# Routed experts: gate and up products as three FP32r products of split operands, with four result buffers

## What is computed

```python
logits = x @ gate_weight.T                   # x: 2048 x 256, 64 experts
...                                          # softmax, best 6 experts of 3 of 8 groups
buf[slot] = x[tok]                           # 64 experts x 96 slots x 256
g = einsum('ech,emh->ecm', buf, Wg)          # Wg, Wu: 64 x 176 x 256
u = einsum('ech,emh->ecm', buf, Wu)
out = einsum('ecm,ehm->ech', silu(g) * u, Wd)
y = sum(out[slot] * topk_w)  +  shared expert
```

## Time and profile before

| | |
|---|---|
| median of 3 runs | 1696.71 us (1686.70 to 1700.94) |
| span of the profiled execution | 1695.7 us, granted TensorE clock 0.932 on average |
| busy, share of the span | TensorE 85%, VectorE 63%, GpSimd 46%, ScalarE 44% |
| moved by DMA | 145.50 MB, mean 86 GB/s |

### The profile page before, as it was taken

How to read it: one execution, slowest core, us unless ns; L and a number is a source line. 1 busy time by engine, 2 the same in 40 slices (tenths; PEclk the granted TensorE clock), 3 DMA queues, 4 the chain that set the end, 5 groups by cost and what they waited for, 6 DMA issues and landing times. The chain is left out here.

```text
span 1695.7 us, 39494 instructions
## 1 busy us (share of the span) xinstructions
PE 1441.4 (85%) x14334; PEld 990.9 (58%) x14334; DVE 1075.4 (63%) x2743; ACT 750.3 (44%) x1786; POOL 773.8 (46%) x741
## 2 busy tenths in 40 slices
PE   6879999448889996888999478877899999998799
PEld 3556656414545554455566356654677777777687
DVE  6852222457876564783222388876998888874888
ACT  5533333254555633553333311125776666752322
POOL 4453332763320000454333466606998888973000
PEclk9989999569999998899999788888999999999899
DMA  8309995631110002514999232200000000000000
GB/s 265 98 14 267 284 266 150 204 96 38 38 38 1 1 1 67 152 40 123 280 296 259 73 87 84 78 4 13 3 16 3 12 7 3 16 3 3 10 19 22
DMA packets 92664, 145.50 MB, mean 86 GB/s; under 512 B 25032, under 2 KB 52528, under 8 KB 92512
## 3 DMA queue, kind: packets, MB, share of 16 engines
q1 hardware_dynamic: 62816, 93.06, 19.1%
q0 software_dynamic: 15360, 37.77, 7.7%
q10 hardware_dynamic: 14336, 12.59, 2.7%
HBM read 122.39 MB, written 18.87 MB: 83 GB/s over the span
## 5 line engine op out<-in xcount | busy, mean ns | idle before, releaser
L2298 POOL TENSOR_TENSOR sb_m_prob<-sb_m_prob,sb_m_rinv 128x512 f32<-128x512 f32 x256 | 260.1, 1041 | 44.6 <-DVE sb_m_rinv L2348 40.8
L1272 POOL DMA_INDIRECT sb_c_rows<-slot_rows,sb_slot x192 | 192.1, 1000 | 102.7 <-issue 51.2
L2228 ACT ACTIVATE sb_m_prob<-m_ps_s,sb_m_nmax 128x512 f32<-128x512 f32 x256 | 173.8, 683 | 125.8 <-DVE sb_m_nmax L2354 125.2
L1106 POOL DMA_INDIRECT e_xn<-xn_rows,sb_table x128 | 117.7, 920 | 209.6 <-PE e_ps_x L1184 197.2
L1255 DVE TENSOR_TENSOR sb_e_h<-sb_e_sg,e_ps_gu 96x176 f32<-96x176 f32 x128 | 42.6, 333 | 256.5 <-ACT sb_e_sg L1231 256.5
L1193 PE MATMUL e_ps_gu<-e_wgu,sb_e_xT 128*96 128x352 f32 x512 | 178.1, 470 | 17.0 <-ACT sb_e_xT L1225 15.6
L2354 DVE TENSOR_REDUCE sb_m_nmax<-m_ps_s 128x1 f32<-128x512 f32 x256 | 163.8, 681 | 28.1 <-PE m_ps_s L2132 25.7
L2362 DVE STREAM_TRANSPOSE sb_m_pT<-sb_m_prob 128x1024 f32<-128x1024 f32 x128 | 157.5, 1232 | 0.0
L2145 PE MATMUL m_ps_v<-sb_m_pT,sb_m_lat_rows 32*64 32x128 f32 x8192 | 136.1, 275 | 4.6 <-issue 3.8
L2131 PE MATMUL m_ps_s<-sb_m_latT_high,sb_m_qa 128*128 128x512 f32 x256 | 125.5, 490 | 16.0 <-ACT sb_m_prob L2228 15.9
L2145 PEld LDWEIGHTS m_ps_v<-sb_m_pT,sb_m_lat_rows 32*64 32x64 f32 x8192 | 120.2, 131 | 27.8 <-issue 27.4
(11 more groups left out here) (280 smaller groups left out, 3076.4 us busy)
## 6 DMA issues: line engine op xcount, KB each, us to landing
e_wgu<-wgu SPq DMA_DIRECT2D x128, 352.0 KB, 4.9
e_wdn<-wdn SPq DMA_DIRECT2D x128, 192.0 KB, 4.7
slot_rows<-sb_e_y ACTq DMA_DIRECT2D x128, 96.0 KB
xn_rows<-e_xn SPq DMA_DIRECT2D x16, 256.0 KB, 2.2
sb_c_rows<-slot_rows,sb_slot POOLq DMA_INDIRECT x192, 2.8
sb_x<-x SPq DMA_DIRECT2D x4, 512.0 KB, 5.4
e_xn<-xn_rows,sb_table POOLq DMA_INDIRECT x128, 5.3
sb_g_zm<-wqT SPq DMA_DIRECT2D x1, 2048.0 KB, 9.1
```

The source lines that it names most:

```text
L1106: pool.indirect_dma_start(x, None, k.xn_rows[:, :], bass.IndirectOffsetOnAxis(ap=k.table[:, e:e + 1], axis=0))\
L1272: pool.indirect_dma_start(rows[u][j][:, :], None, k.slot_rows[:, :], bass.IndirectOffsetOnAxis(ap=k.slot[:, n, j:j + 1], axis=0))\
L2228: act.activation(prob[s % 4][:, hh, :], ps_s[j % 3][:, :], ACT.Exp, bias=nmax[s % 2][:, hh:hh + 1], accum_out=rsum[s % 2][:, hh:hh + 1]).t ...
L2298: pool.tensor_tensor(part, part, rinv[s % 2][:, hh:hh + 1].to_broadcast([P, T]), ALU.mult)\
```

## The change

In the routed experts, the tokens and the gate/up weights are each split into a high part (rounded to FP32r by a ScalarE copy) and a low part (what remains, rounded to FP32r, by a VectorE subtraction). The product becomes three products for each half of the features, high x high, high x low and low x high. The weights of expert s+1 are split in step s, into three buffers of pairs; the wait for the loaded weights goes from TensorE to ScalarE. SyncE may load over a `wgu` buffer once its low part is made. The results `y` have four buffers and four semaphores.

```diff
--- before.py
+++ after.py
@@ -1112,23 +1112,25 @@
 
 
 
-    U, GA, LAG = AHEAD, 4, 3
+    U, GA, LAG, YB, WB = AHEAD, 4, 3, 4, 3
     got = [k.sem(f"e_tokens_got{u}") for u in range(GA)]
     w_got = [k.sem(f"e_weights_got{u}") for u in range(U)]
-    xT_raw, xT_ready = k.sem("e_xT_psum_ready"), k.sem("e_xT_ready")
+    xT_raw, xT_high, xT_low = k.sem("e_xT_psum_ready"), k.sem("e_xT_high_ready"), k.sem("e_xT_low_ready")
+    w_high, w_low = k.sem("e_weight_high_ready"), k.sem("e_weight_low_ready")
     gu_ready, act_ready, h_ready = k.sem("e_gate_up_ready"), k.sem("e_silu_ready"), k.sem("e_hidden_ready")
     hT_raw, hT_ready = k.sem("e_hT_psum_ready"), k.sem("e_hT_ready")
     dn_ready, y_ready = k.sem("e_down_ready"), k.sem("e_y_ready")
-    y_stored = [k.sem(f"e_y_stored{u}") for u in range(2)]
+    y_stored = [k.sem(f"e_y_stored{u}") for u in range(YB)]
     with ExitStack() as ctx:
         sb, ps = scoped(nc, ctx)
         x = k.gathered
-        xT = [sb(f"e{r}_xT{u}", [P, DC, CAP]) for u in range(2)]
+        xTs = [[sb(f"e{r}_xT_{part}{u}", [P, DC, CAP], F32R) for part in ("high", "low")] for u in range(2)]
         wgu, wdn = k.wgu, k.wdn
+        ws = [[sb(f"e{r}_w_{part}{u}", [P, DC, 2 * M0], F32R) for part in ("high", "low")] for u in range(WB)]
         sg = [sb(f"e{r}_sg{u}", [CAP, M0]) for u in range(2)]
         h = [sb(f"e{r}_h{u}", [CAP, M0]) for u in range(2)]
         hT = [sb(f"e{r}_hT{u}", [MH, 2, CAP]) for u in range(2)]
-        y = [sb(f"e{r}_y{u}", [CAP, D]) for u in range(2)]
+        y = [sb(f"e{r}_y{u}", [CAP, D]) for u in range(YB)]
         ps_x = [ps(f"e{r}_ps_x{u}", [P, DC, CAP]) for u in range(2)]
         ps_gu = [ps(f"e{r}_ps_gu{u}", [CAP, 2 * M0]) for u in range(2)]
         ps_h = [ps(f"e{r}_ps_h{u}", [MH, 2, CAP]) for u in range(2)]
@@ -1152,7 +1154,7 @@
         def _(sp):
             def load(e, u):
                 g = e + r * E0
-                sp.wait_ge(gu_ready, g - (U - 1))
+                sp.wait_ge(w_low, g - (U - 1))
                 sp.dma_start(wgu[u][:, :, :], k.w["wgu0"][e]).then_inc(w_got[u], 16)
                 sp.wait_ge(dn_ready, g - (U - 1))
                 sp.dma_start(wdn[u][:, :, :], k.w["wdn0"][e]).then_inc(w_got[u], 16)
@@ -1179,19 +1181,22 @@
                     a = u % GA
                     pe.wait_ge(got[a], (g + (GA - a)) * (16 // GA))
                     if later(s, 2):
-                        pe.wait_ge(xT_ready, g - 1)
+                        pe.wait_ge(xT_low, g - 1)
                     for c in range(DC):
                         ins = pe.transpose(ps_x[v][:, c, :], x[a][:, c * P:(c + 1) * P], k.ident[0:CAP, 0:CAP])
                     ins.then_inc(xT_raw, 1)
                 if live(s, 1):
                     v = (u - 1) % 2
-                    pe.wait_ge(xT_ready, g)
-                    pe.wait_ge(w_got[(u - 1) % U], (lap + (1 if u else 0)) * 32 + loads_of((u - 1) % U) * r)
+                    pe.wait_ge(xT_low, g)
+                    pe.wait_ge(w_low, g)
                     if later(s, 3):
                         pe.wait_ge(h_ready, g - 2)
-                    for c in range(DC):
-                        ins = pe.matmul(ps_gu[v][:, :], xT[v][:, c, :], wgu[(u - 1) % U][:, c, :],
-                                        start=(c == 0), stop=(c == DC - 1))
+                    m = 0
+                    for xpart, wpart in ((0, 0), (0, 1), (1, 0)):
+                        for c in range(DC):
+                            ins = pe.matmul(ps_gu[v][:, :], xTs[v][xpart][:, c, :], ws[(u - 1) % WB][wpart][:, c, :],
+                                            start=(m == 0), stop=(m == 3 * DC - 1))
+                            m += 1
                     ins.then_inc(gu_ready, 1)
                 if live(s, 2):
                     v = u % 2
@@ -1215,6 +1220,10 @@
 
         @block.scalar
         def _(act):
+            def weights_high(w, lap):
+                act.wait_ge(w_got[w], (lap + 1) * 32 + loads_of(w) * r)
+                act.activation(ws[w % WB][0][:, :, :], wgu[w][:, :, :], ACT.Copy).then_inc(w_high, 1)
+
             def step(s, u, lap):
                 g = s + r * E0
                 if live(s, 0):
@@ -1222,7 +1231,11 @@
                     act.wait_ge(xT_raw, g + 1)
                     if later(s, 2):
                         act.wait_ge(gu_ready, g - 1)
-                    act.activation(xT[v][:, :, :], ps_x[v][:, :, :], ACT.Copy).then_inc(xT_ready, 1)
+                    act.activation(xTs[v][0][:, :, :], ps_x[v][:, :, :], ACT.Copy).then_inc(xT_high, 1)
+                if live(s, -1):
+                    if later(s, 2):
+                        act.wait_ge(gu_ready, g - 1)
+                    weights_high((u + 1) % U, lap + (1 if u + 1 == U else 0))
                 if live(s, 1):
                     v = (u - 1) % 2
                     act.wait_ge(gu_ready, g)
@@ -1230,23 +1243,36 @@
                         act.wait_ge(h_ready, g - 2)
                     act.activation(sg[v][:, :], ps_gu[v][:, 0:M0], ACT.Silu).then_inc(act_ready, 1)
                 if live(s, 3):
-                    v = (u - 1) % 2
+                    v, b = (u - 1) % 2, (u - 3) % YB
                     act.wait_ge(dn_ready, g - 2)
-                    if later(s, 5):
-                        act.wait_ge(y_stored[v], (g - (3 + v)) * 8)
-                    act.activation(y[v][:, :], ps_y[v][:, :], ACT.Copy).then_inc(y_ready, 1)
+                    if later(s, 3 + YB):
+                        act.wait_ge(y_stored[b], (g - (3 + b)) * (16 // YB))
+                    act.activation(y[b][:, :], ps_y[v][:, :], ACT.Copy).then_inc(y_ready, 1)
                     act.wait_ge(y_ready, g - 2)
-                    act.dma_start(k.slot_rows.rearrange("(e c) d -> e c d", c=CAP)[s - 3], y[v][:, :])\
-                       .then_inc(y_stored[v], 16)
-
+                    act.dma_start(k.slot_rows.rearrange("(e c) d -> e c d", c=CAP)[s - 3], y[b][:, :])\
+                       .then_inc(y_stored[b], 16)
+
+            weights_high(0, 0)
             pipelined(act, step, U, last, U)
-            for v in range(2):
-                act.wait_ge(y_stored[v], 16 * ((r + 1) * E0 // 2))
+            for b in range(YB):
+                act.wait_ge(y_stored[b], 16 * ((r + 1) * E0 // YB))
 
         @block.vector
         def _(dve):
+            def weights_low(w, g):
+                dve.wait_ge(w_high, g + 1)
+                dve.tensor_tensor(ws[w % WB][1][:, :, :], wgu[w][:, :, :], ws[w % WB][0][:, :, :].bitcast(F32),
+                                  ALU.subtract).then_inc(w_low, 1)
+
             def step(s, u, lap):
                 g = s + r * E0
+                if live(s, 0):
+                    v = u % 2
+                    dve.wait_ge(xT_high, g + 1)
+                    dve.tensor_tensor(xTs[v][1][:, :, :], ps_x[v][:, :, :], xTs[v][0][:, :, :].bitcast(F32),
+                                      ALU.subtract).then_inc(xT_low, 1)
+                if live(s, -1):
+                    weights_low((u + 1) % U, g + 1)
                 if live(s, 1):
                     v = (u - 1) % 2
                     dve.wait_ge(act_ready, g)
@@ -1260,6 +1286,7 @@
                         dve.wait_ge(dn_ready, g - 3)
                     dve.tensor_copy(hT[v][:, :, :], ps_h[v][:, :, :]).then_inc(hT_ready, 1)
 
+            weights_low(0, r * E0)
             pipelined(dve, step, U, last, U)
```

## The result

The changed kernel takes 1671.97 us (median of four runs, 1667.71 to 1680.91), against 1694.12 for the kernel before on the same chip (four runs, 1686.70 to 1700.94). The ratio is 0.9864, with a 95% interval of 0.982 to 0.9909: faster by 0.9 to 1.8%. The forecast was 1667, with a range of 1646 to 1693.

The account below looks back on a forecast made before the run. TensorE, store buffers and transfers were taken to bound the routed experts nearly alike. Afterwards transfers end the first layer at 279.2 us, the loop the second at 936: 16.2 and 13.4 less, 29.6 together, giving 1667 us, range 1646 to 1693.

Parts of the forecast that it names:

- The store wait: ScalarE's result copy in the routed experts: 98.0 us idle for earlier stores, to fall under 15 with four buffers.
- rival 4: Four result buffers don't end ScalarE's store wait; the turn would be 2.6 us; chance 0.18 together with rival 2.
- The loop: Routed experts: a chain through ScalarE, VectorE and TensorE takes 4.61 us per two turns, 2.31 a turn, 150 a layer.
- The transfers: Expert weight loads: DMA already full, last weights land as before; first layer ends at 279.2 us, second could at 933.0.
- The rival that said so (1): Transfers were not the limit, rates pass 300 GB/s, the loop decides both expert layers: 1661 us; chance 0.14.
- landings under 5 us: Weight loads landing this fast show no long DMA queue; cited as evidence that transfers were not the limit.
- the share of 1.0: DMA engines' busy share while expert weights load; cited as evidence that transfers already were at their limit.
- TensorE: Six FP32r gate/up products take 0.97 us in place of 1.18, making TensorE's own turn 2.17 us.
- Rival 2: Gain eaten by FP32r products at 0.235 us whatever their width, or slow splits: 1680 to 1701; 0.18 with rival 4.
- the two splits: Expert weights: ScalarE's rounding 0.79 us (bounds 0.63 to 1.06), VectorE's remainder 0.89 us (bounds 0.35 to 1.215).
- The gather: The gather's issue on POOL stretches above 1.2 us in the mean beside VectorE's weight remainder, hidden from TensorE.
- Rival 3: VectorE's weight remainder waits behind POOL's gather, up to 0.92 us a turn: slower, about 1720 us; chance 0.08.

Follow-up runs that it names:

- kernel 1: The kernel before with four result buffers alone, the gate/up product left in FP32: 1673.35 us, ratio to before 0.9889.
- kernel 3: The changed kernel with VectorE's weight remainder moved behind the hidden product and the hT copy: 1662.76 us, ratio to before 0.9817.
- kernel 7: The changed kernel with ScalarE's issue of the result store moved behind the next turn's weight rounding: 1657.47 us, ratio to before 0.9801.
- kernel 8: The changed kernel with VectorE's weight remainder last in its turn and the result store issued behind the next weight rounding: 1658.03 us, ratio to before 0.9786.
- kernel 2: The changed kernel with two result buffers in place of four, the split kept: 1707.69 us, ratio to before 1.0111.
- kernel 4: The changed kernel with four gate/up products in place of six, low x high left out: 1672.63 us, ratio to before 0.9879.

## Why the prediction came out as it did

**The store wait** went, as forecast (rival 4 falls), and it carries the gain: kernel 1 has it without the split.

**The loop** was right in its path and nearly in its size: 4.61 us forecast, 4.70 measured, the largest difference 0.09 in the piece from hT copy to result copy. Kernels 3 and 7 each take one piece out of it and get a shorter stage. In the second layer this gave 151 us for 154.6 measured: 0.04 us in each of 65 turns are 2.6 of it. The 4.70 is not the same everywhere, as the last section shows.

**The transfers** are the step that failed: "the last weights land where they land now", 279.2 for the end of the first layer. The stage ended at 279.30, but not for that reason: it began 2.2 us later than before and took 154.0 us where 156.1 were forecast, and its last weights were in some 18 us before its end. The match is luck. The loads go out when buffers come free, so a faster loop issues them earlier, and 277 GB/s was what the kernel before asked for, not what can be had: 293 here, 304 in kernel 1, 312 and 340 in windows of kernels 3 and 8. The rival that said so (1) was right in this, and its warning sign, landings under 5 us, was the better one than the share of 1.0. Its time, 1661, didn't come: the stages took 154.0 and 154.6 us where it had 150 and 151, which is 7.6 of the 11 us between; the rest lies outside the stages. The forecast's number was met by a longer loop, not by the transfers. The 2.72 and 2.62 us an expert that the prediction gave the transfers were too long; 2.49 was read in the slow part of kernel 3, and the limit showed only late in the stage there, from about the 45th of 64 turns on, and in the changed kernel never.

**TensorE** came out as forecast: 1.02 us from the first gate/up record at 201.44 to the hidden transposes behind it at 202.46 in kernel 8 (0.97 forecast), and the turn above. Rival 2 falls with it: the products do not cost 0.235 us whatever their width, and the two splits, 0.781 and 0.892 us, are not at their upper ends. What the prediction did not say is that this saving would buy nothing: it never set the loop's 2.31 us against TensorE's 2.38 with FP32, and kernel 1, which has the 2.38, is as fast as the loop's 2.35.

**The gather** was forecast to stretch above 1.2 us and stayed at 0.932. The step that failed is "such an operation and a gather now meet every turn": in the loop shown in the section on the result the gather runs from 202.33 to 203.25 and the remainder starts at 203.59. That they do stretch when they meet, and that only POOL pays, kernel 3 shows (1.328 and 0.878 us). Rival 3 falls there, in the kernel where its condition does arise.

**The whole** is less than the stages: 28.0 us in the profiles, 22.2 in the medians. In every one of the nine kernels the time is 3 to 13 us above what its stages alone would make it, kernel 2 included, whose stages are longer than before. What is outside the stages is the same code; in the ten profiles it takes 1356.0 to 1373.8 us, 1359.1 before and 1370.6 after. Part of the difference lies in the stretch between the two expert layers (windows, before and then changed):

```profile
295.35:784.96 489.61, 379.49 (x2115) 234.19 (x2116) 316.52 (x747) 233.19 (x384) 163.12 (x145) 0.88 0.20 60
```
```profile
279.30:773.93 494.63, 387.68 (x2116) 239.06 (x2116) 316.95 (x747) 233.24 (x385) 163.38 (x145) 0.86 0.20 59
```

The granted clock in such a row is a mean over stretches at 1.00 and at 0.50, that is at 2.4 and 1.2 GHz. Over the ten profiles the stretch takes 489.1 to 489.8 us at 0.88 to 0.89 in the kernel before and in kernels 2 and 4, and 491.4 to 498.0 us at 0.86 to 0.87 in the other seven. In the first three TensorE is busy for 91 to 94% of the first expert stage, in the others for 98% or more. No run tests whether the one follows from the other, and it leaves kernel 2's excess unexplained, so the cause as a whole stays open. There is one profile of the kernel before, and its stages or the rest of it may not be the usual ones.

## What to carry to other kernels

A DMA share of 1.0 is no proof of a limit, nor is a rate that a kernel has reached: ask whether loads land late or whether anybody waits for them, and take half the bytes away to see. Where prefetch runs many tiles ahead, the limit of the transfers shows up at the end of a stage, when the head start is used up, so read turns in its first and last parts apart. Cutting an engine's work pays only if that engine's own turn is the longest; here leaving out a third of the gate/up products took 1 and 2 us off the stages, and moving one DMA issue behind the next operations took off 7 and 12.

## What the runs showed of the hardware

The store's issue on ScalarE is short (0.32 us), yet right behind the result copy it cost 0.78 us of the path in the turns shown (1.06 against 0.28): 0.36 is the issue, the rest lies between the end of the copy that it waits for and the start of the operation behind it. This price isn't constant. In the first eight turns of each layer the way is shorter (changed kernel, timeline):

```profile
784.23 0.38 ACT L1250 ACTIVATE sb_e_y<-e_ps_y 96x256 f32<-96x256 f32 x1
...
785.07 0.33 ACT L1234 ACTIVATE sb_e_xT_high<-e_ps_x 128x192 fp32r<-128x192 f32 x1 [0.46 <-ACT sb_e_y L1250]
```

That is 0.84 us, and these eight turns average 2.27 and 2.24 us in the two layers; later the way is mostly 1.02 to 1.08 us, once in twelve turns 1.4, and from the 11th to the 40th turn the mean is 2.39. In kernel 7 it is 0.28 us in both parts, once in twelve turns 0.5. What makes the later turns longer was not tested.

A gather's issue on POOL was held where a VectorE operation with two SBUF inputs was already running: in kernel 3 such gathers end 1.66 to 1.69 us after the start of that operation, whenever in it they began. Starting just ahead did not save a gather: those that began 0.11 to 0.18 us ahead took 1.78 to 1.85 us and end as late, between 0.23 and 0.28 some took 0.92 and some 1.9, and from 0.29 to 0.47 ahead all took 0.91 to 0.92. VectorE's operation took 0.88 to 0.89 us in every case.

Outside the expert stages time moves with the granted clock. The last stretch, with the same code, in kernels 1 and 3 (windows):

```profile
925.39:1662.00 736.61, 641.32 (x10256) 485.77 (x10256) 593.56 (x1456) 338.70 (x892) 438.90 (x416) 0.95 0.09 25
```
```profile
917.06:1671.90 754.84, 659.41 (x10256) 497.61 (x10256) 596.38 (x1456) 337.84 (x892) 438.83 (x416) 0.92 0.09 24
```

At a mean granted clock of 0.95 it takes 736.6 us, at 0.92 754.8. TensorE was busy for about 98% or more of the expert stage before it in both, at mean clocks of 1.00 and 0.99; why the one execution was granted less than the other is open.
